# First self attention of a decoder kernel: one head's output product in every step of TensorE, in place of two heads' in every second step

## The reference, cut to what matters

```
# _L0_attn_ref: H = 16 heads of D = 128, x is (8, 256, 512)
q  = (x @ Wq.T).reshape(b, n, H, D)
kp, vp = split(x @ Wkv.T)                    # one key and one value row of 128 for all heads
kv_head = cumsum((x @ Wkvh.T) * exp(cumsum(log_sigmoid(x @ Wg.T), shifted)))
kh, vh = split(kv_head)                      # a scalar per token and head
k = kp * kh ; v = vp * vh                    # per head
q, k = rope(q), rope(k)
p = softmax(causal(q @ k.T / sqrt(D)))
o = (p @ v).reshape(b, n, H * D)
x = layernorm(x + o @ Wout.T)                # Wout is (512, 2048): a sum over 16 heads
```

## Time and profile before

| | |
|---|---|
| median of 3 executions | 3309.2 us (3295.82 to 3311.93) |
| profiled execution, its own time | 3292.8 us |
| its span in the trace | 3291.0 us |
| TensorE busy | 2830.0 us (86%) |
| VectorE busy | 2091.4 us (64%) |
| ScalarE busy | 1764.0 us (54%) |
| POOL busy | 1419.4 us (43%) |
| first self attention, scores of step 0 | from 85.19 us |
| first self attention, last output product (step 132) | from 719.10 us |

### The profile page before, as it was taken

The page is one execution under the profiler, slowest core; times in us unless marked ns, Lnnn a source line. Parts: engine busy times, 40 slices in busy tenths (PEclk is TensorE's granted clock), DMA queues, the critical chain, the costliest instruction groups (busy, mean ns, idle before and its releaser), DMA issues. The chain is left out here.

```text
span 3291.0 us, 64401 instructions
## 1 busy us (share of the span) xinstructions
PE 2830.0 (86%) x24866; PEld 2007.4 (61%) x24866; DVE 2091.4 (64%) x4481; ACT 1764.0 (54%) x3844; POOL 1419.4 (43%) x1539
## 2 busy tenths in 40 slices
PE   3999999965888886999999968888999999975786
PEld 1666666643666665777777756666666766652343
DVE  4676776656788775655555547765555565555896
ACT  3555555544887885332233257764444444454785
POOL 0444444423888884544445425451111122212563
PEclk9999999997899997999999989999999999997999
DMA  4000000010000012100000011002000110022000
GB/s 167 1 1 1 1 1 1 1 42 27 2 2 2 2 47 73 46 8 7 1 1 1 1 49 40 21 2 71 14 33 33 39 40 1 1 71 77 14 20 26
DMA packets 45077, 81.49 MB, mean 25 GB/s; under 512 B 5603, under 2 KB 15845, under 8 KB 44646
## 3 DMA queue, kind: packets, MB, share of 16 engines
q1 hardware_dynamic: 44774, 77.38, 6.9%
HBM read 73.18 MB, written 4.19 MB: 24 GB/s over the span
## 5 line engine op out<-in xcount | busy, mean ns | idle before, releaser
L1099 POOL TENSOR_TENSOR c_pT<-c_prob,c_pT 128x512 f16<-128x512 f32 x256 | 296.1, 1172 | 92.4 <-ACT c_pT L1051 90.2
L1974 POOL TENSOR_TENSOR c_prob<-c_prob,c_inv 128x512 f32<-128x512 f32 x128 | 133.4, 1043 | 310.7 <-DVE c_inv L2198 310.7
L754 DVE SCALAR_TENSOR_TENSOR a_pT<-psT,a_kvh_t,a_pT 128x256 f16<-128x256 f32 (+1 forms) x256 | 94.6, 411 | 169.7 <-ACT a_pT L663 169.7
L1099 POOL TENSOR_TENSOR a_pT<-a_prob,a_pT 128x384 f16<-128x384 f32 x128 | 120.8, 950 | 160.0 <-ACT a_pT L1051 159.4
L1371 DVE TENSOR_REDUCE c_peak<-psS 128x2 f32<-128x512 f32 x256 | 171.0, 685 | 29.6 <-PE psS L1202 26.6
L1290 ACT ACTIVATE c_prob<-psT 128x512 f32<-128x512 f32 x256 | 155.2, 607 | 55.7 <-PE psT L1221 35.8
L465 POOL TENSOR_TENSOR a_q_rot<-a_q_cos,a_q_sin 128x512 f32<-128x512 f32 x64 | 81.0, 1266 | 194.6 <-DVE a_q_sin L773 194.6
L1051 ACT CAST c_pT<-c_prob 128x512 f16<-128x512 f32 x256 | 159.1, 622 | 0.0
L2122 ACT CAST c_pT<-psT 128x512 f16<-128x512 f32 x128 | 74.9, 585 | 140.4 <-PE psT L1986 140.4
L484 POOL TENSOR_TENSOR a_prob<-a_prob,a_inv 128x128 f32<-128x128 f32 x128 | 52.3, 409 | 214.3 <-DVE a_inv L747 214.3
L2114 ACT ACTIVATE c_prob<-psS,c_negmax 128x256 f32<-128x256 f32 x256 | 119.4, 475 | 44.3 <-DVE c_negmax L2191 40.5
(11 more groups left out here) (632 smaller groups left out, 11373.7 us busy)
## 6 DMA issues: line engine op xcount, KB each, us to landing
c_feed<-in_L_ffn_w1T SPq DMA_DIRECT2D x16, 512.0 KB, 3.6
c_feed<-in_L_ffn_w2T SPq DMA_DIRECT2D x16, 512.0 KB, 3.5
x_all<-in_x SPq DMA_DIRECT2D x1, 4096.0 KB, 14.3
a_stage<-in_L_attn_WqT SPq DMA_DIRECT2D x8, 512.0 KB, 7.4
a_stage<-in_L_attn_WoutT SPq DMA_DIRECT2D x8, 512.0 KB, 10.0
a_feed<-in_L_xattn_Wq SPq DMA_DIRECT2D x8, 512.0 KB, 3.7
c_feed<-in_L_xattn_Wo SPq DMA_DIRECT2D x8, 512.0 KB, 4.0
c_feed<-in_L_ffn_w3T SPq DMA_DIRECT2D x8, 512.0 KB, 3.6
```

The costliest lines, as they stand in the source:

```text
L754: last = dve.scalar_tensor_tensor(pT[1][:, r, m, m * P:N], T[:, m * N + m * P:(m + 1) * N], kvh_t[:, b % 2, m, H + h:H + h + 1], pT[0][:, ...
L1099: pool.tensor_tensor(pT[1][:, c % NPH, :], prob[:, c % NPX, :], pT[0][:, c % NPH, :], ALU.subtract)\
L1974: pool.tensor_tensor(prob[:, h % NPB, :, :], prob[:, h % NPB, :, :], inv[:, h % NPB, :].rearrange("p (n a) -> p n a", a=1).broadcast_to([P ...
```

## The change

`project` is called once in each step, for head `t-5`, in place of twice in each even step, for heads `t-6` and `t-5`. The instructions, their number and their operands are the same; the product of an even-numbered head moves from an even step to the odd step before it.

```
--- before.py
+++ after.py
@@ -629,9 +629,8 @@
                         turn_k(b, j)
                     for b, j in due(t, AT_Q, TURN_Q):
                         turn_q(b, j)
-                    for lag in (WO + 1, WO):
-                        if t % 2 == 0 and head(t, lag) is not None:
-                            project(head(t, lag))
+                    if head(t, WO) is not None:
+                        project(head(t, WO))
                     if head(t, TURN_P) is not None:
                         turn_p(head(t, TURN_P))
                     for b, n in due(t, AT_X):
```

## The result

The changed kernel takes 3287.05 us (median of 11 executions, 3283.71 to 3291.37), the kernel before 3303.08 us in the same job (11 executions, 3295.82 to 3311.93). The ratio is 0.9956 with a 95% interval of 0.9946 to 0.9966: 0.44% or some 16 us faster, just under the half per cent that the prediction took for the edge of what counts as a difference. Forecast were 3286 us.

A forecast was written before the change was run, and what follows sets the result against it. TensorE bounds the kernel, with 2.6 us of waits per 80.75 us period. Terms 10.4 + 0.2 + 0.7 - 0.4 + 0.2 + 2.5 + 1.4 + 1.1 = 16.1 us, off 3302.5, give 3286 us; range 3271 to 3304.

The forecast's parts named there:

- the sum: Whole kernel: waits that go minus waits that come, a gain of 16.1 us, with no instruction added or removed.
- What bounds: Full period: everything waits for TensorE; 2.6 us of waits by starts, at most 1.66 us by the busy row.
- Odd steps: Turn of the probabilities: waits of 0.33 and 0.73 for line 754 go entirely; 1.30 us of `project` ahead covers them.
- the turn of the step before comes 1.30 us earlier: Even step before an odd one: its earlier turn was claimed as a second cover of the wait for line 754.
- Even steps: Light steps: exponential's read ends 2.87 us after the start, next scores could start at 3.02, work ends at 3.17; no wait.
- The margin: Light even step: 0.15 us to spare between the earliest next scores and the end of the work.
- Steps 6 to 9: Gates' matmuls to scores of step 9: chain stays 10.34 us; step 6 1.30 shorter, step 9 0.57 longer, gain 0.73.
- the third rival: Step 8's last waits fall too, at most the whole 2.6 per period, 6 us more, 3280 us; chance 0.07.
- Step 117: Head 0's `project` waits 0.7 us for line 795's adds; steps 116 and 117 together lose 0.4 us.
- The end: Last steps without queries: 120 to 122 gain 2.5 us, 123 to 126 gain 1.4, the last steps 1.1.
- The median: Whole time: 16.1 us taken off 3302.5, the middle of four known executions, not off the profiled 3292.8; 3286 us.
- The later parts: Sign of being wrong: parts behind the first self attention shift by more than a few microseconds.

The follow-up runs named there:

- turn_first: Changed kernel with `project` behind the turn of the probabilities in odd steps, no longer ahead of it; 3298.81 us, ratio 0.9998.
- odd_pair: Against the changed kernel, two heads' products in odd steps, a sequence's last head alone in its even step, head 0 alone in the next odd; 3327.73 us.
- after_delay: Changed kernel with two copies into an unread tile on ScalarE ahead of the exponential in even steps; 3300.68 us, ratio 0.999.
- late_112: Changed kernel with head 112's output product made in step 118, ahead of head 113's, instead of step 117; 3287.46 us, ratio 0.9943.
- before_again: The kernel before, unchanged, run once more as a kernel of its own; 3302.6 us, ratio 0.9998.
- after_again: The changed kernel, unchanged, run once more for a single execution; 3286.31 us.

## Why the prediction came out right, step by step

The part shrank by 15.84 us where the sum said 16.1. Start to start, before and after, in us:

| steps | before | after | gain | predicted |
|---|---|---|---|---|
| 0 to 15 | 73.79 | 73.69 | 0.10 | 0.2 |
| 16 to 111 (six periods) | 484.47 | 474.00 | 10.47 | 10.4 |
| 112 to 115 | 18.53 | 17.85 | 0.68 | 0.7 |
| 116 and 117 | 9.27 | 9.83 | -0.56 | -0.4 |
| 118 and 119 | 10.90 | 10.73 | 0.17 | 0.2 |
| 120 to 122 | 12.02 | 9.51 | 2.51 | 2.5 |
| 123 to 126 | 14.21 | 12.78 | 1.43 | 1.4 |
| from 127 to the last product's start | 13.09 | 12.05 | 1.04 | 1.1 |

*What bounds.* By starts, 2.6 us of waits stood in a period of 80.75, and 1.75 of them went. The busy row allowed only 1.66 us in 81.00; in the row of after it leaves 0.75 (79.00 - 78.25), where by starts the one gap ahead of step 9 alone is 0.91. The Trainium skill's sentence that TensorE's busy share is a poor measure (Perfetto Trace Analysis, "Identifying the Most-Contended Engine") held for the kernel after too.

*Odd steps.* The waits of 0.33 and 0.73 went entirely, as forecast. The reason given was half wrong: "the turn of the step before comes 1.30 us earlier. Both cover the wait". turn_first shows that the earlier turn covers nothing, and that the 1.30 us ahead of the turn in its own step do it all. The number came out because the other of the two was enough by itself.

*Even steps.* The exponential's end at 2.87 after the step's start did not move, as the sum assumed. The margin is 0.24 where 0.15 was forecast: I took 0.15 us to resume from a turn behind VectorE, and scores behind ScalarE resume in 0.05 to 0.06 (2.92 - 2.86 in odd_pair, 404.15 - 404.09 in after_delay). The prediction itself took 0.05 for the last steps. It erred on the safe side and changed no term.

*Steps 6 to 9.* The chain from the gates' end to the scores of step 9 was held to stay at 10.34; it is 10.35 (431.03 to 441.38 in the rows below). Step 8 takes 441.38 - 437.30 = 4.08, of which 3.17 is work, so the wait forecast at some 0.9 is 0.91:

```profile
431.03 0.28 PE L116 MATMUL psO<-a_pT,a_v 128*128 128x256 f16 x1
...
437.30 0.22 PE L116 MATMUL psS<-a_kT,a_qT 128*128 128x128 f16 x1
...
441.38 0.23 PE L116 MATMUL psS<-a_kT,a_qT 128*128 128x128 f16 x1 [0.75 <-ACT a_prob L673]
```

So the third rival, that the wait of step 8 falls too, did not come: the gap moved from step 7 to step 8 and grew from 0.83 + 0.06 to 0.91.

*Step 117.* The wait on the adds was forecast at 0.7 and is 0.91: the product stands 1.96 after the step's start at 653.29 instead of 1.05. TensorE, the steps' starts 116 to 118 and the product:

```profile
650.12 0.22 PE L116 MATMUL psS<-a_kT,a_qT 128*128 128x128 f16 x1
...
653.29 0.22 PE L116 MATMUL psS<-a_kT,a_qT 128*128 128x128 f16 x1
...
655.25 0.38 PE L116 MATMUL psP<-a_wo,a_qT 128*128 128x512 f16 x1 [0.74 <-DVE ln_r L794]
...
659.95 0.22 PE L116 MATMUL psS<-a_kT,a_qT 128*128 128x128 f16 x1
```

and VectorE's adds, which follow line 753 at once:

```profile
653.76 0.74 DVE L753 SCALAR_TENSOR_TENSOR a_pT<-psT,a_kvh_t,a_pT 128x256 f16<-128x256 f32 x2 [1.01 <-ACT a_pT L662]
654.42 1.28 DVE L794 TENSOR_TENSOR ln_r<-psP,x_all 128x512 f32<-128x512 f32 x2
```

The second row merges two adds. The first by itself is

```profile
654.42 0.68 DVE L794 TENSOR_TENSOR ln_r<-psP,x_all 128x512 f32<-128x512 f32 x1
```

and ends at 655.10, 4.98 after step 116 began (650.12), where the sum had put about 4.9. The product starts 0.15 after that end. It was due at 3.17 + 1.05 = 4.22 and comes at 5.13: the term of the sum was the right wait, the add ended a little later than taken, and the time to resume was left out.

late_112 took this wait away and gained 0.88 where 1.8 was expected. The rotation of the queries on VectorE shows why, in the changed kernel and then in late_112 with the row ahead of it:

```profile
659.66 0.69 DVE L769 TENSOR_TENSOR a_q_cos<-psS,a_rope_q 128x512 f32<-128x512 f32 x1 [0.75 <-PE psS L118]
```

```profile
657.85 0.74 DVE L754 SCALAR_TENSOR_TENSOR a_pT<-psT,a_kvh_t,a_pT 128x256 f16<-128x256 f32 x2 [0.94 <-ACT a_pT L663]
658.51 0.68 DVE L770 TENSOR_TENSOR a_q_cos<-psS,a_rope_q 128x512 f32<-128x512 f32 x1
```

Step 119 starts at 664.91 in the changed kernel and at 663.75 in late_112, both released by the exponential:

```profile
664.91 0.23 PE L116 MATMUL psS<-a_kT,a_qT 128*128 128x128 f16 x1 [1.63 <-ACT a_prob L673]
```

```profile
663.75 0.23 PE L116 MATMUL psS<-a_kT,a_qT 128*128 128x128 f16 x1 [1.35 <-ACT a_prob L674]
```

From the rotation's start to there pass 5.25 and 5.24 us: VectorE's queue from the rotation on sets the end of step 118, in either kernel. With the wait, the rotation waits for TensorE's queries. Without it they are there 1.86 us sooner, but the rotation stands behind line 754 and begins only 659.66 - 658.51 = 1.15 sooner, of which 0.31 is that the whole of late_112 is ahead by then (649.81 against 650.12 for step 116). 0.84 is left, and this is the gain. What holds line 754 itself is the exponential of step 117, whose row maximum stands behind the adds; that follows from the order of the rows in VectorE's list and was not tested by a run.

*The end.* The evened steps are 3.17 (120 to 122), step 123 is 3.16, and the loop of the softmax gives 3.20 to 3.21 (124 to 126), within 0.04 of the forecast. The last term, 1.1, measured 1.04, but the reason given for it, "one head's product instead of two behind the last `pv`", is wrong. In TensorE's timeline the last `pv` before, then the start of step 127 and the last `pv` after:

```profile
718.60 0.27 PE L116 MATMUL psO<-a_pT,a_v 128*128 128x256 f16 x1
```

```profile
692.97 0.23 PE L116 MATMUL psS<-a_kT,a_qT 128*128 128x128 f16 x1 [0.31 <-ACT a_prob L673]
...
702.14 0.28 PE L116 MATMUL psO<-a_pT,a_v 128*128 128x256 f16 x1
```

Behind the last `pv` both kernels have 12 matmuls of `project`, two heads, and their last one starts 2.87 and 2.88 us after it (721.47 and 705.02). What shrank is the way from the start of step 127 to this `pv`: 718.60 - 708.38 = 10.22 us before and 702.14 - 692.97 = 9.17 after. Both kernels have 24 matmuls of `project` on this way, so what went are waits. That the number came out is luck as far as the stated reason goes.

*The median.* The 16.1 were taken off the middle of the known times and not off the profiled execution. That was needed: 3292.8 - 16.1 = 3276.7 is 10 us below what was measured. That the middle, 3302.5, came within 0.6 us of the median measured for the kernel before (3303.08) was in part luck. It lies halfway between 3295.8 and 3309.2, where none of the four known times was. Most later executions are at 3300.0 to 3307.0 us, and the two high ones of the four, 3309.2 and 3311.9, did not come again.

*The later parts.* The prediction named as a sign of being wrong that the later parts shift by more than a few microseconds. In the first pair of profiles the cross attention did, by 9.4. before_again shows the same shift, 7.5 us, without the change, so the sign was badly chosen: it can't tell the change from the granted clock of an execution.

## What to carry to other kernels

When two kinds of extra work alternate, ask for each step what stands ahead of the instruction that waits, not how much work the step has: 1.30 us moved in front of a turn removed a wait of 0.33 to 0.73, and the same 1.30 moved behind it removed nothing. The light step may be made as light as the chain that ends in it allows (2.92 us here, with 3.17 used); one further move of the same kind cost 45 us of the part. And a gain of 16 us is read from the part's own start-to-start distances, since the cross attention behind it moved by 7 to 9 us between executions of one kernel or the other.

## What the hardware showed that was not expected

Executions of one program on one core differ by the granted clock, and in one job they fell into two groups. In its 29 executions of the kernel before, the mean granted clock is either 0.961 to 0.962 or 0.953 to 0.957, and the times are 3289.7 to 3294.0 or 3300.0 to 3306.3 us, with none between. The groups are not as sharp everywhere: in the 30 executions of the same kernel in the two later jobs, on two other chips, only 3293.07 us (0.960) and 3294.72 (0.958) are near the first group, and 3297.84 and 3298.68 (both 0.957) lie between. In the traces of before and after_delay the first cross attention takes 482 and 479 us at a clock of 0.89 and 0.91, and in those of after, before_again and after_again 490 to 492 at 0.87. The row of after_delay (mean clock 0.962):

```profile
724.45:1203.73 479.28, 373.62 (x4908) 272.55 (x4909) 367.38 (x655) 362.29 (x628) 354.62 (x332) 0.91 0.04 13
```

What puts an execution in the one group or the other is not known; it is not the changed lines, since the same kernel shows both.

The time from a releaser's end to the start of the matmul that waited is not one number, in the same part at the same clock: 0.05 to 0.06 us for scores in 16 bits behind ScalarE's read, 0.15 us for a turn of 32 bits behind VectorE. Neither the kind of matmul nor the engine that releases it explains this by itself. A `pv` in 16 bits behind VectorE, in step 127 before the change, starts 0.06 after the end at 709.51 + 0.41 = 709.92:

```profile
709.51 0.41 DVE L761 TENSOR_TENSOR a_qT<-psO,a_qT 128x256 f16<-128x256 f32 x1
...
709.98 0.28 PE L116 MATMUL psO<-a_pT,a_v 128*128 128x256 f16 x1 [0.49 <-DVE a_qT L761]
```

The product of step 117, also 16 bits behind VectorE, took 0.15 (655.10 to 655.25), and a turn of 32 bits at 714.31 before the change started 0.06 after POOL's line 486 ended at 714.25. What sets it stays open.
